# Stores of a two-layer convolution kernel issued by SyncE in place of ScalarE

## The reference

```
x = x + _L0_conv_ref(_gn(x), L0_conv_weight)
x = x + _L1_conv_ref(_gn(x), L1_conv_W1, L1_conv_b1, L1_conv_W2, L1_conv_b2, L1_conv_W3, L1_conv_b3)
```

## Time and profile before

| | us |
|---|---|
| median of 3 runs | 2797.71 |
| lowest and highest of the 3 | 2787.22, 2801.8 |
| profiled execution, its own time | 2791.78 |
| span of its core (first to last instruction) | 2790.1 |
| DVE busy in the span | 2296.2 |
| PE busy | 1993.1 |
| ACT busy | 1661.3 |

### The profile page before, as it was taken

One profiled execution on the slowest core, in us unless ns is written; L12 is line 12 of the kernel. 1 busy time (PEld: TensorE's weight loads), 2 busy tenths in 40 slices (PEclk: granted clock), 3 DMA queues, 4 the chain that ended last, 5 costly groups with the idle time before them and its releaser, 6 DMA issues. The chain is left out here.

```text
span 2790.1 us, 76859 instructions
## 1 busy us (share of the span) xinstructions
PE 1993.1 (71%) x28880; PEld 1881.5 (67%) x28880; DVE 2296.2 (82%) x4175; ACT 1661.3 (60%) x3051; POOL 1167.8 (42%) x1988
## 2 busy tenths in 40 slices
PE   4099887878688777878688776787778787888500
PEld 0089887767677767767677776777767777878500
DVE  6888888899788988899788998889878996958725
ACT  2067666756557565766567565675657666777621
POOL 1032225524435344453455245353544534555433
PEclk9999999999899998999899998999989998999855
DMA  8876848999799988999899998999889996979899
GB/s 253 308 253 220 303 163 339 387 353 341 284 395 366 366 312 325 397 346 372 316 345 385 346 353 298 404 355 366 323 330 383 343 362 235 328 257 329 294 349 345
DMA packets 319770, 915.85 MB, mean 328 GB/s; under 512 B 42864, under 2 KB 42864, under 8 KB 317520
## 3 DMA queue, kind: packets, MB, share of 16 engines
q1 hardware_dynamic: 203744, 595.03, 59.6%
q10 hardware_dynamic: 115840, 318.80, 29.5%
HBM read 594.18 MB, written 319.68 MB: 328 GB/s over the span
## 5 line engine op out<-in xcount | busy, mean ns | idle before, releaser
L1067 PEld LDWEIGHTS psY<-wsplit,XT 128*128 128x128 f16 x25920 | 1608.0, 102 | 366.1 <-issue 123.2
L1067 PE MATMUL psY<-wsplit,XT 128*128 128x168 f16 (+5 forms) x25920 | 1635.9, 223 | 296.4 <-DVE band L730 130.9
L573 ACT CAST XT<-psT 128x512 f16<-128x512 f32 x720 | 414.4, 576 | 560.3 <-PE psT L1053 261.8
L715 DVE TENSOR_TENSOR XT<-psT,XT 128x512 f16<-128x512 f32 x720 | 489.9, 680 | 278.2 <-ACT XT L573 277.3
L743 DVE BATCH_NORM_STATS2 entries<-abuf 128x6 f32<-128x512 f32 x928 | 587.2, 680 | 60.4 <-DMA abuf<-in_x 60.0
L970 POOL TENSOR_TENSOR xn<-xn,mask 128x512 f32<-128x512 f32 x336 | 411.1, 1224 | 499.7 <-ACT xn L558 437.1
L1053 PE MATMUL psT<-ident,xn 128*128 128x128 f32 x2880 | 482.1, 292 | 176.7 <-POOL xn L970 127.0
L1002 POOL TENSOR_TENSOR ubuf<-ubuf,bias 128x1024 f32<-128x1024 f32 x184 | 417.4, 2269 | 435.6 <-ACT ubuf L622 435.5
L993 POOL COPY halo<-XT 128x16 f16<-128x16 f16 x720 | 241.5, 335 | 615.2 <-DVE XT L715 600.7
L1053 PEld LDWEIGHTS psT<-ident,xn 128*128 128x128 f32 x2880 | 318.9, 147 | 189.6 <-POOL xn L970 98.3
L558 ACT ACTIVATE xn<-kept_c_band,normp 128x512 f32<-128x512 f32 (+2 forms) x496 | 398.3, 803 | 44.3 <-DMA kept_c_band<-in_x 26.1
(11 more groups left out here) (77 smaller groups left out, 432.8 us busy)
## 6 DMA issues: line engine op xcount, KB each, us to landing
abuf<-in_x SPq DMA_DIRECT2D x464, 512.0 KB, 7.2
out<-ubuf ACTq DMA_DIRECT2D x288, 512.0 KB, 6.0
kept_c_band<-in_x SPq DMA_DIRECT2D x224, 512.0 KB, 7.9
out<-kept_c_band ACTq DMA_DIRECT2D x224, 512.0 KB, 7.1
ubuf<-in_x SPq DMA_DIRECT2D x192, 512.0 KB, 6.4
band<-in_x SPq DMA_DIRECT2D x48, 1024.0 KB, 8.7
out<-band ACTq DMA_DIRECT2D x48, 1024.0 KB, 10.1
ubuf<-out SPq DMA_DIRECT2D x96, 512.0 KB, 8.2
```

Of the source, the lines that this page charges most:

```text
L573: nc.scalar.copy(XT[:, n % NB3, 0, :, 2:P + 2], psT[n % NB3][:, :, :]).then_inc(hi_ready, 1)
L715: nc.vector.tensor_tensor(XT[:, n % NB3, 1, :, 2:P + 2], psT[n % NB3][:, :, :], XT[:, n % NB3, 0, :, 2:P + 2], ALU.subtract).then_inc(lo_r ...
L1067: last = nc.tensor.matmul(psY[m][:, 0:rows, o + lo_c:o + hi_c], XT[:, m, xp, i, 2 - sh:2 - sh + P], wsplit[:, c, wp, K * sh:K * sh + rows, ...
```

## The change

The three functions that issue stores move from ACT's program to SP's, and with them their places in a stage: at position n SP first issues the position's loads, then the position's spills, kept halves and streamed units, in the order in which ACT had them. What each store waits for stays the same, except that the wait is an instruction of its own (`wait_alone`). ACT keeps the four edge copies and, at the end of the program, the waits for the last stores.

```diff
@@ SP's stage @@
                         if n == NEXT_BIAS_LOAD:
                             load_bias(gb, 0)
+                        for i, at in spill_pos.items():
+                            if at == n:
+                                spill(gb, i)
+                    if do_c:
+                        for blk in KEPT:
+                            for h in range(2):
+                                if kept_pos[blk][h] + 1 == n:
+                                    store_kept(gc, blk, h)
+                        for u in range(NU):
+                            if p.u_store[u] == n:
+                                store_stream(gc, u)
+
+            def spill(g, i):
+                c, b, q = LOWER[i]
+                wait_alone(sp, evicted, NT * g + last_tile[LOWER[i]] + 1)
+                sp.dma_start(ov[chan(g, c), b][:, :, BW * q:BW * (q + 1)], transit[b][:, :, BW * q:BW * (q + 1)]
+                              ).then_inc(x1_spilled[(b, q)], 16)
+
+            def store_kept(g, blk, h):
...
+                wait_alone(sp, kept_done, NR * g + 2 * i + h + 1)
+                sp.dma_start(part(ov[chan(g, c), b], blk, half * h, half), part(kept[(c, b)], blk, half * h, half)
+                              ).then_inc(kept_stored[(blk, h)], 16)
+
+            def store_stream(g, u):
...
+                wait_alone(sp, u_finished if on_dve[u] else u_added, of[NU] * g + of[u] + 1)
+                sp.dma_start(part(ov[chan(g, c), b], STREAM[u]), unit_of(ubuf, u % NUB, STREAM[u])
+                              ).then_inc(u_stored[u % NUB], 16)
@@ ACT's functions @@
-            def spill(g, i):
-                c, b, q = LOWER[i]
-                act.wait_ge(evicted, NT * g + last_tile[LOWER[i]] + 1)
-                act.dma_start(ov[chan(g, c), b][:, :, BW * q:BW * (q + 1)], transit[b][:, :, BW * q:BW * (q + 1)]
...
-            def store_kept(g, blk, h):
...
-            def store_stream(g, u):
...
@@ ACT's stage @@
-                        for i, at in spill_pos.items():
-                            if at == n:
-                                spill(gb, i)
...
-                        for blk in KEPT:
-                            for h in range(2):
-                                if kept_pos[blk][h] + 1 == n:
-                                    store_kept(gc, blk, h)
-                        for u in range(NU):
-                            if p.u_store[u] == n:
-                                store_stream(gc, u)
```

More of the change, by code:

```diff
@@ L484, in stage @@
                             load_bias(gb, 0)
+                        for i, at in spill_pos.items():
[15 more added lines that the diff above has]
+            def store_kept(g, blk, h):
+                c, b = blk[:2]
+                half = blk[5] // 2
+                i = KEPT.index(blk)
+                wait_alone(sp, kept_done, NR * g + 2 * i + h + 1)
+                sp.dma_start(part(ov[chan(g, c), b], blk, half * h, half), part(kept[(c, b)], blk, half * h, half)
+                              ).then_inc(kept_stored[(blk, h)], 16)
+            def store_stream(g, u):
+                c, b = STREAM[u][:2]
+                of = u_before[on_dve[u]]
+                wait_alone(sp, u_finished if on_dve[u] else u_added, of[NU] * g + of[u] + 1)
+                sp.dma_start(part(ov[chan(g, c), b], STREAM[u]), unit_of(ubuf, u % NUB, STREAM[u])
+                              ).then_inc(u_stored[u % NUB], 16)
             def load_kept(g, blk, h):
@@ L597, in piece @@
                                      bias=col(cur, 3), accum_out=squares[:, j:j + 1]).then_inc(pieces_done, 1)
-            def spill(g, i):
-                c, b, q = LOWER[i]
-                act.wait_ge(evicted, NT * g + last_tile[LOWER[i]] + 1)
-                act.dma_start(ov[chan(g, c), b][:, :, BW * q:BW * (q + 1)], transit[b][:, :, BW * q:BW * (q + 1)]
-                              ).then_inc(x1_spilled[(b, q)], 16)
-            def store_kept(g, blk, h):
[L606 to L611, removed]
             def shift_bias(g, c, columns):
```

## The result

| | before | after |
|---|---|---|
| median, us | 2798.81 | 2834.65 (2828.40 to 2840.57, 4 runs) |
| ratio | | 1.0136, interval 1.0099 to 1.0172 |
| span of the profiled execution, us | 2790.1 | 2826.7 |

A forecast was written before the change was run, and what follows sets the result against it. It took laps to be bound closely by DVE and transfers, through a chain of store, landing, load, landing, use. Laps gain 30 us, stages 8 and 9 lose 13, so 2797.7 - 17 = 2781 us, range 2748 to 2826.

The forecast's parts named there:

- SP's side, gains in a full lap: Four gains from moved stores; the first, a unit's store at the lap's end, 2 us a lap, between 0 and 3.4.
- Kept half, 3 us a lap: In a full lap, a kept half's store no longer delayed by loads SP issued ahead; gain 3 us, between 0 and 5.
- Spill, 2 us: In a full lap, a spill lands sooner with three 512 KB loads behind it; gain 2 us, between 0 and 4.5.
- Others, 1 us: The same gain at a lap's other kept halves and units; 1 us, between 0 and 2.
- SP's lead, costed at nothing in the laps: In the laps, loads now behind stores go later but were taken to land in time; loss 0.
- rival 3: Slower: five places a lap where SP's lead is missed, 3.1 us each; 2858 us at most, some 2830; chance 0.14.
- The sign named for it: In the changed profile's laps, DVE's waits for `abuf` and ACT's for `ubuf` grow; no size given.
- Stage 8, 4 us: One run of stores and loads in each of two windows becomes a chain; loss 4 us.
- Stage 9, 9 us: Last stage: loads wait behind stores on SP; loss 6 us in the second half, 3 us in the first.
- ACT's relief, nothing: ACT loses 560 store issues and its stops at stores; gain taken as nothing.
- Rival 4: Slower: at the lap's end, stores lose their queue's turn and stand behind 1024 KB of loads; 2822 us; chance 0.12.
- Rival 2: No change: DMA share of 0.95 in laps means the bytes set the time; 2797 us; chance 0.32.

The follow-up runs named there:

- e8: Kernel before, with only streamed units' stores of positions 76 to 89, in stages with step A, moved to SP; ratio 1.0052.
- e16: Kernel before, with ACT storing POOL-finished units right behind the position's cast, only from position 76 on; ratio 0.9965.
- e5: Changed kernel's stores on SP only in stages 0 to 7, on ACT in stages 8 and 9; ratio to the kernel before 1.0065.
- e13: Kernel before, with ACT waiting for POOL-finished units right behind the cast but issuing their stores at the position's end as before; ratio 1.0015.
- e7: Changed kernel, with ACT's waits for store results put back at the old places, without the DMAs; ratio to the kernel before 1.0113.
- e4: Kernel before, all stores still on ACT, but SP also waits for the same results where the changed kernel has the stores; ratio 1.0078.
- e11: Kernel before, with ACT storing POOL-finished units right behind the position's cast instead of at the position's end; ratio 0.9885.
- e14: Changed kernel, with stores of POOL-finished units ahead of the position's loads on SP, the others behind them; ratio to the kernel before 1.0026.
- e10: Changed kernel, with SP's loads and stores merged in order of the issue times in the trace of before; ratio to the kernel before 1.0204.
- e9: Changed kernel, with SP's stores merged among loads by when their results were ready in the trace of before; ratio to the kernel before 1.0052.
- e6: Changed kernel, with every store on SP ahead of its position's loads; ratio to the kernel before 1.0145.
- e15: Kernel before, with ACT storing all units and spills right behind the cast, kept halves at the position's end; ratio 1.0007.

## Why the prediction was wrong

**The step that failed** is the first of "SP's side, gains in a full lap": "On SP the store would go after one load more, about 2.4 us earlier", with "later links give some back. I take 2 us". I had read ACT's lateness at one unit and taken SP to be free. For that unit it held (e8: 1.1 us in place of 3.4). But SP is not free, and the mean lateness of unit stores stayed at 2.29 us. Worked out from the records of after, the 216 stores are 494 us late in sum; in 193 of these SP stands for the landing of another unit's store (that is, in front of a load), in 69 for DVE's statistics of an `abuf` unit, and in 28 for a kept half. The prediction had read the first of these waits in the earlier trace rows but not the second, the largest of all (745.5 us before). The links behind gave back more than everything: the tail alone cost 15 us. The size of 2 us a lap for prompt stores came out near: e16, which has all of POOL's unit stores from position 76 on early, gained 10 us in six laps and the two stages behind them. What failed was that moving a store to SP makes it prompt. The prediction's last sentence names a stall of SP that delays several loads at once as what would make it wrong most easily, but no term of the sum has a price for it.

**Kept half, 3 us a lap:** wrong. It was to wait less behind SP's loads; the landing is 7.2 in place of 7.1 us, and the kept halves alone cost 0.65%. **Spill, 2 us:** landing 10.2 in place of 10.1 us, alone 0.15% slower, which is hardly more than nothing. **Others, 1 us:** no sign of it, and no run tests it alone. In place of -30 us the laps and what is ahead of them took +13.0 us in the profiled executions, and +18 in e5's ratio.

**SP's lead, costed at nothing in the laps:** wrong, and at the very load of the earlier trace rows, unit 6's. I had given it the median of 6.4 us to its landing. In the trace of before it had itself taken longer (the load of 1436.50):

```profile
DMA to landing us min/median/max: 11.9/11.9/11.9
```

It landed at 1448.41, 7.3 us ahead of its use. After:

```profile
1452.96 0.44 SPq L515 DMA_DIRECT2D out<-ubuf  x1
1453.52 0.40 SPq L474 DMA_DIRECT2D ubuf<-in_x  x1
...
1466.06 1.15 ACT L640 ACTIVATE ubuf<-ubuf,outp 128x1024 f32<-128x1024 f32 x1 [5.38 <-DMA ubuf<-in_x]
```

It now goes right behind the store, as foreseen, lands 12.5 us later, and ACT stands for it for 5.38 us. Unit 4, a few positions earlier, had 3.6 us from landing to use and ran out of them as well. So rival 3's condition, loads that land over 8 us after issue, was met at this load already in the kernel before; only the median (6.4 us, unchanged) hid it. The sign named for it did come: ACT's waits for units, 303.6 in place of 140.1 us.

**Stage 8, 4 us:** right, 4 measured in one execution each (before and e13 differ by 2 there). **Stage 9, 9 us:** the mechanism was right, the size was not: 19.5 us, some 9 in the first half (3 forecast) and some 10.5 in the second (6 forecast). Both together are 23.5, inside the bound of 25 (four legs). ACT stood 23.4 us for one unit, which the first half had as one half of a leg, 3 us. The timeline there:

```profile
2654.84 11.03 SPq L508 DMA_DIRECT2D out<-kept_c_band  x5
2665.95 0.39 SPq L515 DMA_DIRECT2D out<-ubuf  x1
...
2668.97 1.27 DVE L899 SCALAR_TENSOR_TENSOR ubuf<-ubuf,outp,bias 128x1024 f32<-128x1024 f32 x1
...
2673.72 1.22 SPq L474 DMA_DIRECT2D ubuf<-in_x  x1
...
2680.13 1.15 ACT L640 ACTIVATE ubuf<-ubuf,outp 128x1024 f32<-128x1024 f32 x1 [23.37 <-DMA ubuf<-in_x]
```

The load of 2673.72 is unit 4's and needs only that unit 0's store has landed. POOL finished unit 0 at 2658.15, but its store stands behind five stores of kept halves in one row and goes at 2665.95, 7.8 us late (1.5 before); it landed at 2669.57. The load goes 4.2 us later still, since in SP's program it also stands behind three more kept halves and the stores of units 1 to 3, the last of which DVE finishes at 2670.24. Here it was not one leg that was added, but DVE's pace put ahead of the loads.

**ACT's relief, nothing:** right (e7). **Rivals:** rival 3, SP's lead missed (0.14), is the nearest: e4 has only that mechanism and makes 22 of the 38 us. Rival 3's own terms, though, give 2843 with half of the laps' gain; its "some 2830" takes all of it. Rival 4, the store's own queue turn, can have no more than what lies between e4 and e7, 0.35%, which the two intervals leave open from nothing to some 0.7%, and shares it with the stores' place behind SP's loads. Rival 2's "bytes bind" is refuted: e11 moves the same bytes in 32 us less. None of them, nor the forecast, had it that ACT's lateness costs tens of us where it is and could be had without moving anything.

## What to carry to other kernels

Before moving a store to another engine, write down for a whole lap, and not for one store, what stands ahead of it in the new program and when that becomes free, with the engine's largest waits first; for a load that loses its lead take its own time to landing, not the median; a wait for a result that is put ahead of loads turns side-by-side transfers into a chain, and costs most where nothing else is left to do, at the program's end. Read the lateness of stores (result ready to issue) and the slack of loads (landed to used): both are cheap to read, and here a plain reordering inside the issuing engine, of those stores alone whose results are there or nearly so, gave 1.3% where the move took 1.4%. Move no store ahead of work that is ready while its own result is not.

## What was not expected of the hardware

Three pairs of kernels that differ in the lateness of unit stores (the third in that of kept halves and spills too) come near to one price for it in spite of different engines and queues: e13 to e11, 2.37 to 0.80 us, 36 us of time (1.0015 - 0.9885); after to e14, 2.29 to 0.63, 31 us; e10 to e9, 2.56 to 0.49, 42 us. That is 19 to 23 us for 1 us of mean lateness over 216 stores of the laps, about a tenth of the sum of the delays. It is no law: e6 against after and e15 against e13 cut 1.2 and 1.8 us of lateness and gain nothing and 2 us, since they hold loads or ACT. And a store of 512 KB landed after 4.5 us or 13.6 us at the same place of the program, with two or eight other transfers on their way when it was issued.
